# A state-space loop with drive, scan and product in one SBUF ring, both channel halves in one instruction

## The reference

```python
xz = x @ W_in + b_in
x_proj, z = jnp.split(xz, 2, axis=-1)      # 256 channels each
u = _silu(x_proj)
A = -jnp.exp(A_log)                        # 256 x 16
x_dbl = u @ W_x + b_x
Bm, Cm = jnp.split(x_dbl, 2, axis=-1)      # 16 states each
dt = jax.nn.softplus(u @ W_dt + b_dt)

def step(h, inp):                          # over the 128 tokens
    u_t, dt_t, B_t, C_t = inp
    dA = jnp.exp(dt_t[..., None] * A)
    h = h * dA + (dt_t * u_t)[..., None] * B_t[:, None, :]
    y_t = jnp.einsum('bds,bs->bd', h, C_t) + D_param * u_t
    return (h, y_t)
...
y = y * _silu(z)
return y @ W_out + b_out
```

## Time and profile before

| | us |
|---|---|
| median of three runs | 362.44 |
| lowest, highest | 362.34, 363.05 |
| the profiled execution | 363.72 |
| its span on the core | 361.6 |
| VectorE busy in the span | 298.3 (82%) |
| TensorE (matmul) busy | 312.2 (86%) |
| GpSimd busy | 188.1 (52%) |
| ScalarE busy | 214.9 (59%) |
| mean granted TensorE clock | 0.968 of full speed |

### The profile page before, as it was taken

The page is one execution under the profiler, slowest core; times in us unless marked ns, Lnnn a source line. Parts: engine busy times, 40 slices in busy tenths (PEclk is TensorE's granted clock), DMA queues, the critical chain, the costliest instruction groups (busy, mean ns, idle before and its releaser), DMA issues. The chain is left out here.

```text
span 361.6 us, 5633 instructions
## 1 busy us (share of the span) xinstructions
PE 312.2 (86%) x1750; PEld 236.5 (65%) x1750; DVE 298.3 (82%) x743; ACT 214.9 (59%) x504; POOL 188.1 (52%) x225
## 2 busy tenths in 40 slices
PE   8858396798998998699777989897899989999993
PEld 5646395696665747444446855575698658989873
DVE  0899999997988898999999999999949334844945
ACT  4666323233255867579488548797556566765742
POOL 2499997664514053878768797968404600100111
PEclk9989689999999999899989999999999999999998
DMA  8920000000000004454443435344100000000011
GB/s 227 418 100 2 1 0 3 0 1 2 0 2 1 0 4 147 122 158 153 140 137 128 162 106 171 129 132 133 58 2 0 2 0 1 3 0 2 1 31 29
DMA packets 11668, 24.44 MB, mean 68 GB/s; under 512 B 1247, under 2 KB 2399, under 8 KB 11383
## 3 DMA queue, kind: packets, MB, share of 16 engines
q1 hardware_dynamic: 11639, 24.09, 20.0%
HBM read 23.50 MB, written 0.59 MB: 67 GB/s over the span
## 5 line engine op out<-in xcount | busy, mean ns | idle before, releaser
L1070 POOL TENSOR_TENSOR arena<-arena 128x512 f32<-128x512 f32 x63 | 81.0, 1289 | 34.0 <-DVE arena L741 30.4
L741 DVE TENSOR_TENSOR_SCAN arena<-arena,ps 128x512 f32<-128x512 f32 x64 | 77.3, 1209 | 0.1
L1341 ACT ACTIVATE arena<-arena,neg_a 128x508 f32<-128x508 f32 x64 | 43.4, 714 | 6.9 <-DVE arena L741 6.8
L734 DVE TENSOR_TENSOR ps<-arena,ps 128x512 f32<-128x512 f32 x64 | 43.3, 678 | 1.9 <-PE ps L1787 1.9
L769 DVE TENSOR_REDUCE arena<-ps 128x2 f32<-128x496 f32 x32 | 21.4, 667 | 24.8 <-PE ps L1849 24.8
L1803 PE MATMUL ps<-first_in,arena 128*128 128x128 f32 x256 | 40.0, 280 | 1.2 <-POOL arena L1070 1.1
L1115 POOL TENSOR_TENSOR rstd<-veps,mhalf 128x4 f32<-128x4 f32 (+2 forms) x6 | 5.0, 838 | 67.5 <-DVE veps L843 35.5
L1803 PEld LDWEIGHTS ps<-first_in,arena 128*128 128x128 f32 x256 | 32.7, 145 | 10.5 <-issue 3.3
L1787 PE MATMUL ps<-arena,pick_wide 96*128 96x512 bf16 x64 | 25.1, 397 | 15.6 <-DVE arena L741 14.8
L1618 PE MATMUL ps<-arena,first_in 128*128 128x128 f32 (+1 forms) x192 | 25.7, 295 | 10.6 <-POOL arena L966 10.6
L1618 PEld LDWEIGHTS ps<-arena,first_in 128*128 128x128 f32 x192 | 24.7, 209 | 13.0 <-POOL arena L966 12.8
(11 more groups left out here) (287 smaller groups left out, 768.5 us busy)
## 6 DMA issues: line engine op xcount, KB each, us to landing
arena<-c_rows_dram SPq DMA_DIRECT2D x64, 256.0 KB, 3.2
fold_in<-in_fold_dram SPq DMA_DIRECT2D x1, 2056.0 KB, 11.0
late_in<-in_late_dram SPq DMA_DIRECT2D x1, 1423.5 KB, 16.9
early_in<-in_early_dram SPq DMA_DIRECT2D x1, 921.5 KB, 12.8
xres<-in_x_dram SPq DMA_DIRECT2D x1, 512.0 KB, 13.6
kv_ctx<-in_context_dram SPq DMA_DIRECT2D x1, 480.0 KB, 6.8
rows_in<-in_rows_dram SPq DMA_DIRECT2D x1, 384.0 KB, 14.1
first_in<-in_first_dram SPq DMA_DIRECT2D x1, 320.0 KB, 5.1
```

Source lines behind the costliest of these rows:

```text
L734: tt(chain(q), dtu[:, n, cols(g)], chain(q), ALU.mult).then_inc(S("drive"), 1)
L741: nc.vector.tensor_tensor_scan(hist[:, q % NBUF], fade[:, q % NFADE], chain(q), 0.0, ALU.mult, ALU.add).then_inc(S("scan"), 1)
L1070: tt(seen[:, q % NBUF], hist[:, q % NBUF], c_wide[:, q % NBUF], ALU.mult).then_inc(S("read_out"), 1)
L1341: act(fade[:, q % NFADE].rearrange("p (b t) -> p b t", t=T)[:, :, 1:], dt[:, n, cols(g)].rearrange("p (b t) -> p b t", t=T)[:, :, 1:], ACT ...
```

## The change

A step of the loop becomes one state with both channel halves side by side: 32 states, with instructions of 2 x 512 columns. The first four states (`LEAD`) still go half by half, so there are 8 half-width and 28 full-width items. B and C of one state are stored as neighbouring rows in DRAM (a permutation of the columns of W_x and b_x on the host's layout) and come in one broadcast DMA of two rows into `bc_wide` (four buffers). Only for the first two states B is widened by a matmul with a column of the identity matrix, as fp32, into PSUM. The drive goes into a slot of a ring of five in SBUF (`hist`), the scan runs in place there, and so does the product with C; TensorE transposes out of that slot. The three bf16 parts of B, `pick_wide` and `seen` are gone. Each of the four y blocks has its own PSUM bank, and several attention steps change banks. The y blocks of a batch half leave together, behind its 16th state. `dtu` of the last two blocks is made by one instruction. The second step softplus (`softplus(1)`) moves ahead, between fades 3 and 4 on ScalarE.

```diff
-        NFADE, NBUF = 6, 4
-        fade = A(NFADE * HW).rearrange("p (n t) -> p n t", n=NFADE)
+        NFADE, NRING, NWIDE = 4, 5, 4
+        fade = A(NFADE * NH * HW).rearrange("p (n h t) -> p n h t", n=NFADE, h=NH)
...
-        hist = A(NBUF * HW).rearrange("p (n t) -> p n t", n=NBUF)
-        seen = A(NBUF * HW).rearrange("p (n t) -> p n t", n=NBUF)
-        c_wide = A(NBUF * HW).rearrange("p (n t) -> p n t", n=NBUF)
+        hist = A(NRING * NH * HW).rearrange("p (n h t) -> p n h t", n=NRING, h=NH)
+        bc_wide = A(NWIDE * 2 * HW).rearrange("p (n k t) -> p n k t", n=NWIDE, k=2)
...
+        ITEMS = [(d, n, n + 1) for n in range(NH) for d in range(LEAD)] + [(d, 0, NH) for d in range(LEAD, ND)]
...
+        def both(ap):
+            return ap.unsqueeze(1).to_broadcast([P, NH, HW])
...
-                sp.dma_start(c_rows[:, cols(g)], bc_f[NS:2 * NS, cols(g)]).then_inc(S(f"c_stored{g}"), 16)
-                for q in range(g * NK4, (g + 1) * NK4):
-                    sp.wait_ge(S(f"c_stored{g}"), 16)
-                    if q >= NBUF:
-                        sp.wait_ge(S("read_out"), q - NBUF + 1)
-                    sp.dma_start(c_wide[:, q % NBUF], c_rows[q % NS, cols(g)].partition_broadcast(P)).then_inc(S(f"c_wide{q % NBUF}"), 16)
+                sp.dma_start(bc_rows[g], bc_f[0:2 * NS, cols(g)]).then_inc(S(f"bc_stored{g}"), 16)
+                for d in range(g * NS, (g + 1) * NS):
+                    s = d % NS
+                    sp.wait_ge(S(f"bc_stored{g}"), 16)
+                    if d >= NWIDE:
+                        sp.wait_ge(S("read_out"), through(d - NWIDE))
+                    if d < 2:
+                        sp.dma_start(wide(d, 1), bc_rows[g, 2 * s + 1].partition_broadcast(P)).then_inc(S(f"bc_wide{d % NWIDE}"), 16)
+                    else:
+                        sp.dma_start(bc_wide[:, d % NWIDE], bc_rows[g, 2 * s:2 * s + 2].partition_broadcast(P)).then_inc(S(f"bc_wide{d % NWIDE}"), 16)
...
-            def drive_of(q):
-                g, n, s = at_step(q)
-                ve.wait_ge(S("b_mm"), q + 1)
-                if s == 0 and q:
-                    ve.wait_ge(S("dtu_ready"), q // NS)
-                tt(chain(q), dtu[:, n, cols(g)], chain(q), ALU.mult).then_inc(S("drive"), 1)
-
-            def scan_of(q):
-                ve.wait_ge(S("fade"), q + 1)
-                ve.wait_ge(S("drive"), q + 1)
-                if q >= NBUF:
-                    ve.wait_ge(S("read_out"), q - NBUF + 1)
-                nc.vector.tensor_tensor_scan(hist[:, q % NBUF], fade[:, q % NFADE], chain(q), 0.0,
+            def drive_of(i):
+                d, first, last = ITEMS[i]
+                at = cols(d // NS)
+                if d >= NRING:
+                    ve.wait_ge(S("seen_used"), through(d - NRING))
...
+                if d < 2:
+                    ve.wait_ge(S("b_mm"), d + 1)
+                    tt(slot(d)[:, first], dtu[:, first, at], bank(1 + d), ALU.mult).then_inc(S("drive"), 1)
+                elif last - first == 1:
+                    ve.wait_ge(*wide_ready(d))
+                    tt(slot(d)[:, first], dtu[:, first, at], wide(d, 0), ALU.mult).then_inc(S("drive"), 1)
+                else:
+                    ve.wait_ge(*wide_ready(d))
+                    tt(slot(d), dtu[:, :, at], both(wide(d, 0)), ALU.mult).then_inc(S("drive"), 1)
+
+            def scan_of(i):
+                d, first, last = ITEMS[i]
+                ve.wait_ge(S("fade"), i + 1 if i < 2 * LEAD else 2 * (d + 1))
+                ve.wait_ge(S("drive"), i + 1)
+                state = slot(d)[:, first:last].rearrange("p h t -> p (h t)")
+                nc.vector.tensor_tensor_scan(state, fade[:, d % NFADE, first:last].rearrange("p h t -> p (h t)"), state, 0.0,
                                              ALU.mult, ALU.add).then_inc(S("scan"), 1)
...
+            for q in range(2 * LEAD, NQ, 2):
+                i = item_at(q)
+                if i + 1 < NI:
+                    drive_of(i + 1)
+                between(q)
+                scan_of(i)
+                between(q + 1)
...
+            def seen(i):
+                d, first, last = ITEMS[i]
+                po.wait_ge(S("scan"), i + 1)
+                po.wait_ge(*wide_ready(d))
+                if last - first == 1:
+                    tt(slot(d)[:, first], slot(d)[:, first], wide(d, 1), ALU.mult).then_inc(S("read_out"), 1)
+                else:
+                    tt(slot(d), slot(d), both(wide(d, 1)), ALU.mult).then_inc(S("read_out"), 1)
...
+            for f in range(LEAD):
+                fading(f)
+            table_of(ACT.Softplus)
+            softplus(1, 6)
+            table_of(ACT.Exp)
+            for f in range(LEAD, NH * LEAD):
+                fading(f)
...
+            for d in range(2):
+                mm(bank(1 + d), ident[0:2 * NS, 2 * d:2 * d + 1].to_broadcast([2 * NS, P]), bc_f[0:2 * NS, cols(0)],
+                   start=True, stop=True).then_inc(S("b_mm"), 1)
+            for n in range(NH):
+                ins = steps(1, 6, n)
+            ins.then_inc(S("dt_mm"), 1)
...
+                for n in range(first, last):
+                    for b in range(HB):
+                        ins = mm(y_bank(d // NS * NH + n)[:, b * T:(b + 1) * T], slot(d)[:, n, b * T:(b + 1) * T], ident,
+                                 is_transpose=True, start=False, stop=d % NS == NS - 1 and b == HB - 1)
```

More of the change, by code:

```diff
@@ L143, in decoder @@
         neg_a = sb("neg_a", [P, NH, NS])
-        arena = sb("arena", [P, 27000])
+        arena = sb("arena", [P, 28000])
         ps = ctx.enter_context(nc.psum_tensor("ps", [P, 8 * BANK], F32))
@@ L344, in query_bank, with latent_bank @@
         def query_bank(g, h):
-            return bank(7 if g == 0 and h >= 4 else 6 + h % 2)
+            return bank((6 if g else 1) + h % 2)
+        def latent_bank(g):
+            return bank(7 if g else 3)
         def within_chunk(tt, c):
@@ L778, in normal5, with between @@
                 tt(pr, pr, s5_rden[:, u % 2].unsqueeze(2).to_broadcast([P, 2, KV]), ALU.mult).then_inc(S("prob5"), 1)
[L780 to L785, removed]
-                    landed(3, 1, 7)
[L787 to L792, removed]
+            def between(q):
+                if q == 3:
+                    landed(3, 1, 7)
+                if q == NK4 + 3:
                     gate_turned(0)
-                if q == NK4 + 3:
                     gate_turned(1)
@@ L804, in _ @@
                         shift(u)
-            last = NQ - 1
-            ve.wait_ge(S("scan"), NQ)
-            ve.wait_ge(*c_ready(last))
-            ve.wait_ge(S("seen_used"), last - NBUF + 1)
-            tt(seen[:, last % NBUF], hist[:, last % NBUF], c_wide[:, last % NBUF], ALU.mult).then_inc(S("read_last"), 1)
+            drive_of(0)
+            for i in range(2 * LEAD):
+                drive_of(i + 1)
+                scan_of(i)
+                between(i)
+            for q in range(2 * LEAD, NQ, 2):
+                i = item_at(q)
+                if i + 1 < NI:
+                    drive_of(i + 1)
+                between(q)
+                scan_of(i)
+                between(q + 1)
+            last = ND - 1
+            ve.wait_ge(S("scan"), NI)
+            tt(slot(last), slot(last), both(wide(last, 1)), ALU.mult).then_inc(S("read_last"), 1)
             def add5(b):
@@ L1039, in _, with step_input @@
             residual_half(4, 0, row_in[:, ROWS.index("b_out")])
-            def step_input(m):
-                h = cols(m // 2)
-                po.wait_ge(S("dt"), m + 1)
-                tt(dtu[:, m % 2, h], dt[:, m % 2, h], u4[:, m % 2, h], ALU.mult).then_inc(S("dtu_ready"), 1)
-            STEP_INPUTS = {11: 1, 27: 2, 35: 3}
+            def step_input(first, last):
+                h = cols(first // NH)
+                po.wait_ge(S("dt"), last)
+                n = slice(first % NH, (last - 1) % NH + 1)
+                tt(dtu[:, n, h], dt[:, n, h], u4[:, n, h], ALU.mult).then_inc(S("dtu_ready"), 1)
+            def seen(i):
[6 more added lines that the diff above has]
+                    tt(slot(d), slot(d), both(wide(d, 1)), ALU.mult).then_inc(S("read_out"), 1)
             def latent_scale(g):
@@ L1063, in scaled_latents @@
                        ALU.add).then_inc(S("kv_lat"), 1)
-            for q in range(NQ - 1):
-                po.wait_ge(S("scan"), q + 1)
-                po.wait_ge(*c_ready(q))
-                if q >= NBUF:
-                    po.wait_ge(S("seen_used"), q - NBUF + 1)
-                tt(seen[:, q % NBUF], hist[:, q % NBUF], c_wide[:, q % NBUF], ALU.mult).then_inc(S("read_out"), 1)
-                if q in STEP_INPUTS:
-                    step_input(STEP_INPUTS[q])
-                if q == 2:
+            for q in range(NQ - 2):
+                if q < 2 * LEAD or q % 2 == 0:
+                    seen(item_at(q))
+                if q == 0:
+                    step_input(1, 2)
+                if q == 24:
+                    step_input(2, 4)
```

(9 more changed lines are left out.)

216 lines of the change are left out of this document (87 added, 129 removed).

## The result

The changed kernel takes 428.21 us (median of four runs, 426.88 to 429.53), against 362.50 for the kernel before on the same chip: a ratio of 1.1809, 95% interval 1.1765 to 1.1854. The profiled execution took 429.02 with a span of 427.2. Forecast were 422.5, with 412 to 446 as range.

What follows compares the result with a forecast made beforehand. VectorE was taken to bound the loop. Loop +59.4 us from engines taking turns, start -0.55 and end +1.2 made +60 on the median of 362.44: 422.5 us, range 412 to 446.

Steps and rivals of the forecast that it cites:

- The step that decides: In the loop, drive, scan and product, all reading two SBUF operands, take turns: 5.44 us a state against 3.42; chance 0.83.
- Scan let off: Rival for the loop: the scan takes no turn, only the drive collides; 3.33 us a state, 359.5 in all; chance 0.12.
- Broadcast the bound: Rival for the loop: the 512 KB broadcasts of B and C set the pace if landing doubles, 374 us; chance 0.03.
- No collision: Rival for the loop: VectorE and GpSimd never collide, leaving just the shorter VectorE chain, 357.7 us; chance 0.02.
- the two fast rivals: Loop rivals: the scan takes no turn (359.5 us, chance 0.12), or nothing collides at all (357.7 us, chance 0.02).
- the other GpSimd work: In the loop, step inputs, latent scalings and residuals that read two SBUF tensors take turns as well: 7.9 us.
- The sum: Loop total: 152.3 + 21.8 - 1.1 + 7.9 + 2 = 182.9 us, against 123.5 before.
- in-between work: VectorE's other loop work, 10.2 us after the change, can run in GpSimd's turns; 2 us of it was counted.
- the half items: The loop's first four states go as eight half-width items of 2.73 us each, 21.8 us.
- Start and end: First drive 0.55 us earlier; after the loop 1.2 us more, as the third and fourth y blocks leave together.
- A sign that was wrong: Sign expected in the loop if the forecast held: GpSimd and VectorE both near 100% busy.
- TensorE's clock: TensorE, thinner in the loop, may be granted its lower clock there for a time, off the path in the loop.

## Why the prediction was right

**The step that decides** held: a scan with two SBUF inputs takes turns with GpSimd's product. The two records of 4.43 and 2.28, the fill in the product's place (2.28 wherever no other GpSimd read lies beside the scan) and the operand in PSUM (2.29 beside a product) show it from three sides. Turns of 1.09, 2.14 and 2.21 were to give 5.44 a state; 5.47 was measured. The undisturbed scan of 1,024 columns, taken from the earlier trace rows, is exactly the 2.28.

**The rivals.** *Scan let off*: scans would be constant and the period 3.3 to 3.6; neither is so. *Broadcast the bound*: a row of DMA issues of the changed kernel gives the landing of 512 KB,

```profile
arena<-bc_rows_dram SPq DMA_DIRECT2D x30, 512.0 KB, 3.6
```

3.6 against 3.2 in the earlier trace rows, where a state of 3.33 would have left 4.3 and one of 5.44 leaves 12; one wide drive alone waited for it (1.10). *No collision* fell with the first. The prices of the two fast rivals, 359.5 and 357.7, were too low: the run without products, with no turn left but for the other GpSimd work, took 374.27.

**The mis-sized terms** lie in the loop. The span grew by 65.6 instead of 60: the loop took 189.1 instead of 182.9, and the start gave 0.6 more back. The sum had 2 us for what VectorE does or waits for in between. VectorE's waits in the loop alone come to 14.7. And not all of its in-between work could run in GpSimd's turns: L448, with `mv` as its only input, took 1.21 beside a product that ended at 247.69, against 0.17 in the run without products:

```profile
142.72 0.69 DVE L743 TENSOR_TENSOR arena<-arena 128x512 f32<-128x512 f32 x1 [4.13 <-DMA arena<-bc_rows_dram]
...
246.51 1.21 DVE L448 TENSOR_SCALAR lat_rstd<-mv 128x4 f32<-128x4 f32 x1
...
254.47 3.54 DVE L753 TENSOR_TENSOR_SCAN arena<-arena 128x1024 f32<-128x1024 f32 x1 [2.25 <-ACT arena L1358]
...
320.91 0.68 DVE L781 TENSOR_REDUCE arena<-ps 128x2 f32<-128x496 f32 x1 [3.61 <-PE ps L1861]
```

The waits are 4.13 for the first broadcast of two rows, whose queue the prediction looked at only in the steady part; 1.10 for a later one; 2.25 for a fade; 5.3 in all for row scores from TensorE and 2.0 for ScalarE's part of the attention. None of them had a price.

By VectorE's records the 189.1 us are: wide drives and scans 28 x (3.87 + 1.45 - 0.15) = 144.8 (records overlap by 0.08 and 0.07), the last product 1.2, the half items 17.7, waits 14.7, and, as the rest, 10.7 of in-between work. The sum had 159.1 for the states with the last product and the other GpSimd work, where 146.0 came; 21.8 for the half items, where 17.7 came (four of their eight drives read PSUM and take no turn); and 2 for waits and in-between work, where 25.4 came. The 13.1 that the states took less mostly go with the 25.4: a product that ran on while VectorE waited or did something else held the next scan for less. So 12.3 stayed uncovered, where the sum had 2. That the half items gave back 4.1 of the difference is luck.

**Start and end.** The first drive came 1.15 earlier: 0.56 of it was already there when the step softplus began (134.52 against 135.08 in the earlier trace rows), so the change's own share is 0.59, against 0.55. The two fp32 broadcasts ahead of it left four records and took 1.98 us, not the 1 us that the prediction gave them from the four records in the earlier trace rows; they ended at 136.39, still ahead of the second drive, so it cost nothing. The end was to cost 1.2 and did (102.15 against 100.95).

**A sign that was wrong.** GpSimd was to be near 100% busy in the loop. It was busy for 124.4 of 189.1 us, and idle before 20 products for 46.8 in all, each time until a scan ended. A product cannot stand in line during the scan whose result it needs. GpSimd waits there for a semaphore and not for a turn, so that the scan's turn shows as idle time, and the product's record holds only the drive's. The sum of turns is the same, but the sign would have misled a reader who looked for it.

**TensorE's clock** did fall in the loop (between 170 and 210 us, where TensorE was busy for 23.8 of 40, the mean grant was 0.67, between its levels of 1.2 and 2.4 GHz), and off the path, as argued: with 0.97 the period was the same.

## What to carry to other kernels

Before an operand moves from PSUM to SBUF, look at what GpSimd does beside the instruction: an extra SBUF operand made three instructions on two engines run in series, and cost 2 us a state where the wider form could save 0.1. When two engines take turns, the order decides who pays; read from the durations who was held, and set the order with a wait, since one wait more was worth 19.5 us here. And a record that varies by the length of an instruction of another engine is a wait, though the profile counts it as busy.

## What the runs showed that was not expected

A start 0.01 us ahead was enough where both engines were free: with the product ahead the drive took 3.42, and with the product made to wait for the drive's end 1.23 (5.90 and 3.71 a state). It does not always decide. In the run without products the step input started at 188.25 during a drive, 0.06 ahead of the scan, and yet it was the step input that was held, while the scan took its 2.28; why is not shown. GpSimd's fill of 128x1024 took 0.95 us, against 2.35 for its product, and neither held nor was held. An fp32 matmul of 512 columns took two records and 1.12 us, against 0.40 for bf16. And more work on TensorE raised its grant from 0.67 to 0.97 and made the kernel slower all the same.
